# One bank of the feed-forward rows' transposes a group of value products later, and 42 transposes of the identity at the start

## The reference

```python
x = L0_attn_X                                    # (8, 2048, 256)
x = x + attention(layernorm(x), W_Q, W_K, W_V)   # xpos rotation of Q and K, softmax of all 2048 scores,
                                                 # the probabilities times 0.9 ** |n - m|, times V
x = x + ffn(layernorm(x), w_gate, w_up, w_down)
# ffn: fp4_linear(silu(fp4_linear(x, w_gate)) * fp4_linear(x, w_up), w_down), hidden width 704
# fp4_linear quantises both operands in blocks of 16 to the E2M1 grid, then multiplies
```

## Time and profile before

| | |
|---|---|
| median of three runs | 2640.75 us |
| the profiled execution: its time, its span | 2646.61 us, 2644.8 us |
| mean granted TensorE clock | 0.995 of full |
| PE busy (matmul) | 2578.5 us, 97% |
| PEld busy (weight load) | 2310.8 us, 87% |
| DVE busy | 2151.9 us, 81% |
| POOL busy | 1851.8 us, 70% |
| ACT busy | 1516.3 us, 57% |

### The profile page before, as it was taken

One profiled execution on the slowest core, in us unless ns is written; L12 is line 12 of the kernel. 1 busy time (PEld: TensorE's weight loads), 2 busy tenths in 40 slices (PEclk: granted clock), 3 DMA queues, 4 the chain that ended last, 5 costly groups with the idle time before them and its releaser, 6 DMA issues.

```text
span 2644.8 us, 51900 instructions
## 1 busy us (share of the span) xinstructions
PE 2578.5 (97%) x16146; PEld 2310.8 (87%) x16146; DVE 2151.9 (81%) x4784; ACT 1516.3 (57%) x2966; POOL 1851.8 (70%) x1919
## 2 busy tenths in 40 slices
PE   8999999999999999999999999999999999999997
PEld 7888878988998889988998889888998899888987
DVE  8999878878888788878888788878887888878886
ACT  5666555556565555556555555555555555555554
POOL 6999947666766666767766676666676776667665
PEclk9999999999999999999999999999999999999999
DMA  7777510121111311121112111131113111211110
GB/s 278 282 282 271 192 35 29 33 91 56 39 37 41 105 35 41 38 98 41 41 33 90 58 39 37 41 105 33 43 35 99 42 41 33 87 60 39 37 37 21
DMA packets 163479, 203.37 MB, mean 77 GB/s; under 512 B 15184, under 2 KB 116752, under 8 KB 163216
## 3 DMA queue, kind: packets, MB, share of 16 engines
q1 hardware_dynamic: 163216, 200.01, 23.2%
HBM read 103.42 MB, written 77.59 MB: 68 GB/s over the span
## 4 chain that ended last, share of the span: by engine, by line
PE 80%; DVE 4%; issue 1%; ACT 1%; POOL 1%; DVEq 0%; POOLq 0%
PE score L463 26%; PE ring L463 18%; PE acc L587 18%; PE acc L463 9%; PE ring L556 5%; PE ring L605 3%; DVE smax L1137 2%; DVE xqT L1124 1%; PE acc L627 1%; PE ring L547 1%; ACT xqT L723 0%; DVE nmax L1140 0%; POOL h_buf L932 0%; DVE hT L1124 0%; POOL h_buf L926 0%
## 5 line engine op out<-in xcount | busy, mean ns | idle before, releaser
L463 PE MATMUL score<-keys,q_st 128*128 128x512 f32 x3072 | 773.2, 401 | 18.0 <-issue 11.9
L463 PEld LDWEIGHTS score<-keys,q_st 128*128 128x128 f32 x3072 | 562.8, 190 | 135.7 <-issue 16.9
L911 POOL TENSOR_TENSOR probs<-probs,decay 128x512 f32<-128x512 f32 (+3 forms) x416 | 454.4, 1105 | 179.3 <-ACT probs L753 179.3
L587 PE MATMUL acc<-vals,pT 128*128 128x256 f32 x3984 | 534.4, 285 | 1.6 <-DVE pT L1124 1.6
L1137 DVE TENSOR_REDUCE smax<-score 128x1 f32<-128x1024 f32 x256 | 313.4, 1224 | 245.8 <-PE score L463 244.2
L463 PE MATMUL ring<-w_gu,xqT 128*128 128x512 f32 (+1 forms) x2304 | 509.2, 375 | 0.0
L587 PEld LDWEIGHTS acc<-vals,pT 128*128 128x128 f32 x3984 | 494.6, 189 | 8.1 <-DVE pT L1124 3.3
L723 ACT ACTIVATE pT<-ring 128x512 fp32r<-128x512 f32 (+3 forms) x432 | 226.4, 534 | 453.0 <-PE ring L556 445.4
L463 PEld LDWEIGHTS ring<-w_gu,xqT 128*128 128x128 f32 x2304 | 419.3, 188 | 62.6
L1124 DVE TENSOR_TENSOR pT<-ring,pT 128x512 fp32r<-128x512 f32 (+3 forms) x432 | 250.9, 606 | 68.9 <-ACT pT L723 67.8
L917 POOL TENSOR_TENSOR xv<-xv,xe 128x256 f32<-128x256 f32 x128 | 93.8, 733 | 277.1 <-DVE xv L993 277.1
(11 more groups left out here) (128 smaller groups left out, 4544.7 us busy)
## 6 DMA issues: line engine op xcount, KB each, us to landing
k_dram<-keys SPq DMA_DIRECT2D x56, 512.0 KB, 4.6
keys<-k_dram SPq DMA_DIRECT2D x56, 512.0 KB, 7.5
edge<-vals SPq DMA_DIRECT2D x288, 64.0 KB, 2.0
q_raw<-q_dram SPq DMA_DIRECT2D x129, 128.0 KB, 2.6
x_in<-X SPq DMA_DIRECT2D x32, 512.0 KB, 4.5
q_dram<-q_stage SPq DMA_DIRECT2D x32, 512.0 KB, 5.6
x_res<-X SPq DMA_DIRECT2D x128, 128.0 KB, 2.0
out<-x_res SPq DMA_DIRECT2D x128, 128.0 KB, 1.7
```

Source lines behind the costliest of these rows:

```text
L463: mm = pe.matmul(dst, stat(a, k), mov(m, k), start=i == 0, stop=ends and i == n - 1)
L587: mm = pe.matmul(pv_out, pT[g % 2][:, a, j * P:(j + 1) * P], edge[place][:] if kb in edges else vals[m][:, kb, :], start=i == 0, stop=i == ...
L911: op = pool.tensor_tensor(probs[:, k0:k1], probs[:, k0:k1], decay[:, off + k0:off + k1], ALU.mult)
```

## The change

The second bank of the `hT` transposes goes one group of value products later on TensorE: in a short step bank 0 still follows the first group and bank 1 now follows the second; in a long step they follow the second and the third. The order of banks in the ring stays. VectorE's function is split in the same way, in unchanged order. At the start `ident` is loaded first, and TensorE makes 30 transposes of the identity into the third ring bank before the transposes of the first chunk and 12 after them; nobody reads them.

```diff
+WARM = (30, 12)
...
-            if g == max(len(gs) - LATER, 0) and has(s - LAG):
-                take("hT", s - LAG, 0)
-                take("hT", s - LAG, 1)
+            for h in range(2):
+                if g == min(max(len(gs) - LATER, 0) + h, max(len(gs), 1) - 1) and has(s - LAG):
+                    take("hT", s - LAG, h)
...
+            sp.dma_start(ident[:], eye).then_inc(ident_in, 16)
             chunk_x(0, 1, 0, False)
             for i, w in ((1, WK), (0, WQ), (2, WV)):
                 sp.dma_start(w_raw[:, i * KT * D:(i + 1) * KT * D].rearrange("p (k n) -> p k n", k=KT),
                              w.rearrange("(k p) n -> p k n", p=P)).then_inc(wqkv_in[i], 16)
-            sp.dma_start(ident[:], eye).then_inc(ident_in, 16)
             chunk_x(0, 1, 1, False)
...
+            def warm(n):
+
+                for i in range(n):
+                    pe.transpose(ring[2][:, 0:P], ident[:], ident[:])
+
             pe.wait_ge(ident_in, 16)
+            warm(WARM[0])
             chunk_x(0, 0)
+            warm(WARM[1])
...
-                    if g == max(len(gs) - LATER, 0):
-                        later()
-
-            def h_transposed(at, t):
-                if has(at, t):
-                    pe.wait_ge(hq_ready, tile(at, t) + 1)
-                    for h, ks in enumerate((range(0, CT), range(CT, HK))):
+                    for h in range(2):
+                        if g == min(max(len(gs) - LATER, 0) + h, len(gs) - 1):
+                            later(h)
+
+            def h_transposed(at, t, h):
+                if has(at, t):
+                    for ks in (range(0, CT), range(CT, HK))[h:h + 1]:
+                        if h == 0:
+                            pe.wait_ge(hq_ready, tile(at, t) + 1)
                         dst = slot(at, "hT", t, h)
...
-                attend(at, s - 1, lambda: x_transposed(at, s - 2), lambda: h_transposed(at, s - LAG))
+                attend(at, s - 1, lambda: x_transposed(at, s - 2), lambda h: h_transposed(at, s - LAG, h))
...
-                h_transposed(at, s - LAG)
+                for h in range(2):
+                    h_transposed(at, s - LAG, h)
```

More of the change, by code:

```diff
@@ L566, in attend @@
                     meanwhile()
-                    later()
+                    later(0)
+                    later(1)
                     return
@@ L1150, in attend, with h_transposed @@
                     lower(pT[g % 2][:, 1, 0:n], bank(at, "pT", t, g)[:, 0:n], pT[g % 2][:, 0, 0:n], at, "pT", t, g)
-            def h_transposed(at, t):
+            def h_transposed(at, t, h):
                 if has(at, t):
-                    for h, n in enumerate((CT, HK - CT)):
+                    for n in (CT, HK - CT)[h:h + 1]:
                         hi, lo = (hT[i][:, h * CT:h * CT + n, :].rearrange("p k t -> p (k t)") for i in range(2))
```

## The result

The changed kernel takes 2598.26 us in the median of four runs (2595.02 to 2599.60), the kernel before 2641.32 us in four runs beside them; the ratio is 0.9833, 95% interval 0.9816 to 0.9850. The gain is 43 us, where 34 was forecast: the direction was right, and the time lies just under the range, which began at 2600.

The account below looks back on a forecast made before the run. TensorE, busy 97% of the span, was taken to bound the kernel. Terms -33.8 -1.9 +0.7 +1.0 = -34.0 us, from 2640.75, gave 2606.7 us; range 2601 to 2613 (chance 0.66), wider range 2600 to 2620.

Parts of the forecast that it names:

- The wait of L605: TensorE's 76 waits at the hidden-row transposes for VectorE's xqT would go: gain 33.8 us, bounds 26 and 34.
- The next entry ... is not touched: Six "issue" waits at the scores, at ends of loop iterations on TensorE, 11.9 us, were taken to stay.
- What is late next: Later bank 1 delays ScalarE's exponentials 0.7 us in short steps, 1.1 in long; cost at value products 1.0 us.
- The first rival: VectorE's lateness partly reaches the value products, 0.2 us more in each of 76 steps: 2622, typically 2618 us; chance 0.13.
- the second (a delay counted twice, 2717): Delay through ScalarE's Silu and again through GpSimd's decays makes VectorE 2.8 or 2.2 us late: 2717 us; chance 0.03.
- The fourth: The wait only moves: bank 1 free, but pT2 or gate/up late by the same amount: 2639 us; chance 0.03.
- The beginning: Identity transposes raise TensorE's clock at the start, so the first twelve products run faster: gain 1.9 us, bounds 0 and 2.5.
- the third rival: Identity transposes do not raise the clock, first products start 1.7 us later at the old pace: 2610.3 us; chance 0.15.
- the rule of the Trainium skill: TensorE's full clock does not engage for transposes, so the 42 would raise nothing and the first products stay slow.
- The last step: After it the chain goes through VectorE, which comes no sooner, so its stall gives nothing back: plus 0.7 us.

Follow-up runs that it names:

- the two kernels with 84 increments: 84 increments of an unused semaphore at TensorE's start, in the kernel before (2632.13 us) and in that with only the hT bank moved (2602.02 us).

## Why the prediction was right or wrong

**The wait of L605: right in its cause, 3 us too large.** The wait is gone. Counted between the starts of the six transposes, what goes beyond 0.11 us for each comes to 32.8 us before and 1.8 after, so 31 us were won. Away from batch ends the two kernels draw apart by 0.27 to 0.69 us in each short step, and not at all in long ones. The medians of the two kernels with 84 increments give 30. The weight-load row, 33.8, was thus somewhat too high, as the prediction's bounds of 26 and 34 allowed.

**"The next entry ... is not touched": wrong, and this is the step that failed.** I read "issue" as a fixed cost of the loop. Counted between starts of matmuls the six waits came to 12.9 us, and the change removes them all by shifting TensorE's code; a few tenths to 1.1 us for keys take their place. Without these 12.9 the changed kernel would have taken 2611, inside the range. The runs that part the two add up: early ident and 42 transposes, with what they do at the jumps, 14.1 (2642.95 to 2628.84), the move without waits at the jumps 30.1 (2632.13 to 2602.02), together 44.2, beside 43.1 and 44.1 measured. Both halves of the row's price were open to the change: where the code lies, and how much other traffic the fetch meets. In the prediction's terms, it put this row at nothing without a reason. I had costed the 42 transposes as time on the array and not as 84 instructions, and so had no rival for a better time than the forecast; this, more than the width of any term, put the result below the range.

**What is late next: right.** In a long step the exponentials begin 2.56 us after bank 0 where they began 1.43 after it: 1.13 later, against 1.1.

```profile
995.62 0.60 PE L616 MATMUL ring<-ident,hq_buf 128*128 128x128 f32 x4
...
997.48 0.38 PE L616 MATMUL ring<-ident,hq_buf 128*128 128x128 f32 x2
...
998.18 1.11 ACT L764 ACTIVATE probs<-score,nmax 128x1024 f32<-128x1024 f32 x1
```

VectorE's slack shrinks by the amount forecast: its waits for the scores at the maxima fall from 244.2 us in 203 cases to 126.5 in 134, that is 0.9 us in each of 128 steps.

```profile
DVE smax L1148 <- PE score L464: 126.5, 134, 6.2
```

And it costs nearly nothing: waits of value products for pT are 3.7 us where they were 2.9, so the 1.0 charged is 0.8. The first rival (partial giveback) and the second (a delay counted twice, 2717) therefore fell: long steps did not grow, so the delays through ScalarE and GpSimd do not add. The fourth, a wait that only moves, fell too.

**The beginning: right in sum, and the third rival fell.** The early `ident` landed 1.8 us after its issue; 1.7 was read off the stores. The first chunk's transposes came 0.28 later, against 0.5. The second chunk's came at 17.38, against 17.44 and 19.22 before, and behind them the two kernels stand 2.1 us apart, against the 1.9 of the sum. The clock was raised by transposes alone. The profile's clock column does not show it, since it reads 1.00 until the first recorded change, but the length of a transpose does: the first row is of 3.4 to 8.4 us, the second of 9.1 to 9.45, with nothing else on the array before. From start to start it is 0.21 us until 8.7 and 0.11 from 8.9 on.

```profile
L505 PE MATMUL ring<-ident 128*128 128x128 f32 x24 | 5.4, 423 | 3.3 <-DMA ident<-eye 3.3
```

```profile
L505 PE MATMUL ring<-ident 128*128 128x128 f32 x4 | 0.6, 273 | 0.0
```

By the rule of the Trainium skill weighed in the prediction the transposes would not have done this; the trace disagrees, these float32 transposes do. One thing I had not seen: the 12 are there to keep the clock, and without them it falls before the first products.

**The last step** was charged 0.7 us. The two kernels are 52.0 us apart at the beginning of the last step with scores and 51.9 at the end, so its stall is not won and nothing else is lost: right.

## What to carry to other kernels

An "issue" wait at a loop's backward jump is not a constant. It depends on where the engine's code lies (here 64 to 128 instructions more removed it and 256 brought it back), and on what the DMA engines carry at that moment; so any edit that adds or removes instructions ahead of the loop can move the time by as much as the edit itself, and a control with that many idle instructions tells the two apart. When a step that ends at such a jump is made shorter, ask what transfers it now meets.

## What the hardware showed that I had not expected

- 84 idle instructions ahead of the loop are worth 13 us of 2640 here (six jumps, 1.9 to 2.6 us each). With the moved bank the same jumps cost 21.8 us; there 64 are enough, and 256 bring the cost back.
- A wait at a jump can cost more than its length: around the three longest of those 21.8 us TensorE's clock fell to 1.2 GHz for 3.4 to 6.8 us.
- The fetch behind a jump waits for bulk DMA: halving 4 MB of key loads took 13 us off six jumps. The block's own packet took 1.05 us early or late.
- Transposes of float32 raise TensorE's clock from the 1.2 to the 2.4 GHz level by themselves: 423 ns each until 8.4 us, 273 after 9.1, one every 0.21 us and then every 0.11.
- Semaphore increments are not free on TensorE's sequencer: with 128 of them the first transpose came at 20.5 us, with 256 at 40.3, so (40.3 - 20.5) / 128 = 0.15 us each.
